# The four value products of an attention step side by side

## The reference, cut to what matters

```
def _attn(x, ln_w, ln_b, conv_w, attn_w, proj_w, n_head):   # B=4, T=512, C=128, 16 heads of 8
    h = layernorm(x); h = causal_depthwise_conv(h)
    q, k, v = split(h @ attn_w); q, k = rope(q), rope(k)
    scores = q @ k.T / sqrt(8)
    scores = where(causal, scores, -1e30)
    p = softmax(scores)
    return (p @ v) @ proj_w
```

## Time and profile before

| | |
|---|---|
| median of 3 runs | 2071.69 us (2069.89 to 2074.51) |
| the profiled execution | 2067.15 us, of which the span 2065.4 us |
| PE busy | 1799.8 us, 87% of the span |
| DVE, ACT, POOL busy | 1536.7, 1335.5 and 655.4 us |
| mean granted TensorE clock | 0.944 |
| value products, L1362 | 1024 records, first at 1032.9, last at 1908.2 us |

### The profile page before, as it was taken

How to read it: one execution, slowest core, us unless ns; L and a number is a source line. 1 busy time by engine, 2 the same in 40 slices (tenths; PEclk the granted TensorE clock), 3 DMA queues, 4 the chain that set the end, 5 groups by cost and what they waited for, 6 DMA issues and landing times.

```text
span 2065.4 us, 24716 instructions
## 1 busy us (share of the span) xinstructions
PE 1799.8 (87%) x8806; PEld 1111.0 (54%) x8806; DVE 1536.7 (74%) x2489; ACT 1335.5 (65%) x2121; POOL 655.4 (32%) x735
## 2 busy tenths in 40 slices
PE   8999798888988889997798889997577678988998
PEld 5888466665666657885233335783122233332786
DVE  6888687787877758888766654875999866764786
ACT  6999577676776688997356565555544445566554
POOL 1444211011110013444523321322699442233131
PEclk9999999999999989998799998998899879999999
DMA  3221000000000002220000000200000000000110
GB/s 102 76 78 49 19 19 18 1 18 19 19 18 1 11 11 84 75 69 31 0 1 1 1 1 9 85 21 0 11 3 33 0 1 1 1 1 1 57 56 21
DMA packets 23770, 52.89 MB, mean 26 GB/s; under 512 B 2336, under 2 KB 6816, under 8 KB 23648
## 3 DMA queue, kind: packets, MB, share of 16 engines
q1 hardware_dynamic: 23648, 51.30, 7.8%
HBM read 49.66 MB, written 1.64 MB: 25 GB/s over the span
## 4 chain that ended last, share of the span: by engine, by line
PE 60%; DVE 20%; ACT 15%; issue 3%; POOL 1%; DMA 1%; SPq 0%; POOLq 0%; DVEq 0%; ACTq 0%
PE ps L554 9%; PE ps L556 9%; PE ps L555 9%; PE ps L1362 5%; DVE arena L1986 5%; PE ps L1331 4%; PE ps L786 3%; PE ps L783 3%; DVE arena L1703 2%; PE ps L784 2%; ACT arena L1502 2%; PE ps L1320 2%; PE ps L1350 2%; ACT arena L1451 2%; DVE arena L1977 1%
## 5 line engine op out<-in xcount | busy, mean ns | idle before, releaser
L665 DVE TENSOR_TENSOR hid_lo<-arena,hid_hi 128x512 fp32r<-128x512 f32 x384 | 341.6, 902 | 67.5 <-ACT arena L614 65.5
L1703 DVE TENSOR_REDUCE arena<-ps 128x1 f32<-128x512 f32 (+3 forms) x352 | 219.2, 641 | 82.5 <-PE ps L1335 78.9
L1502 ACT ACTIVATE arena<-ps 128x1024 f32<-128x1024 f32 (+3 forms) x256 | 167.6, 703 | 120.9 <-PE ps L1350 120.6
L554 PE MATMUL ps<-x_hi,w_hi 128*128 128x512 f32 x512 | 208.1, 406 | 3.1 <-DVE arena L757 3.1
L556 PE MATMUL ps<-x_hi,w_lo 128*128 128x512 f32 x512 | 203.4, 397 | 0.0
L555 PE MATMUL ps<-x_lo,w_hi 128*128 128x512 f32 x512 | 203.2, 397 | 0.0
L611 ACT ACTIVATE hid_hi<-ps,wslot 128x512 fp32r<-128x512 f32 x256 | 177.3, 693 | 33.8 <-PE ps L556 6.4
L1616 POOL TENSOR_SCALAR_AFFINE_SELECT arena<-arena 128x256 f32<-128x256 f32 x256 | 108.0, 428 | 283.7 <-ACT arena L1502 281.5
L614 ACT ACTIVATE arena<-ps,wslot 128x512 f32<-128x512 f32 x256 | 175.1, 684 | 0.0
L1331 PE MATMUL ps<-arena 128*128 128x512 bf16 (+3 forms) x512 | 138.5, 328 | 41.0 <-DVE arena L1703 12.7
L635 POOL TENSOR_TENSOR x<-x,arena 128x512 f32<-128x512 f32 x64 | 108.4, 1698 | 146.1 <-DVE arena L626 146.1
(11 more groups left out here) (314 smaller groups left out, 4233.7 us busy)
## 6 DMA issues: line engine op xcount, KB each, us to landing
arena<-gates_dram SPq DMA_DIRECT2D x96, 256.0 KB, 3.6
wslot<-pack_a SPq DMA_DIRECT2D x16, 514.5 KB, 3.6
wslot<-pack_b SPq DMA_DIRECT2D x8, 900.5 KB, 4.6
wslot<-pack_c SPq DMA_DIRECT2D x8, 768.0 KB, 4.5
res<-x_in SPq DMA_DIRECT2D x4, 256.0 KB, 5.1
out_dram<-res SPq DMA_DIRECT2D x4, 256.0 KB, 2.8
con<-consts_dram SPq DMA_DIRECT2D x1, 559.0 KB, 4.0
bc_dram<-arena SPq DMA_DIRECT2D x1, 384.0 KB, 3.2
```

The costliest lines, as they stand in the source:

```text
L554: pe.matmul(ps[:, bank, :], w1, hi, start=start, stop=False)
L665: dve.tensor_tensor(hid_lo[item % 2][:, k, :], hid32[:, k, :], hid_hi[item % 2][:, k, :].bitcast(F32), ALU.subtract).then_inc(S["hid_ok"], 1)
L1502: act.activation(pt[:, u % NPT, :, 0:n], ps[:, 2 * r:2 * r + 2, 0:n], ACT.Exp, scale=SCALE).then_inc(S["exp_ok"], 1)
L1703: dve.tensor_reduce(neg_max[:, i, heads[0]:heads[-1] + 1:step], ps[:, bank, 0:len(heads) * keys].rearrange("p (m k) -> p m k", k=keys), AX ...
```

## The change

Before, a step ran: scores pair, first quarter of sides, scores pair, second quarter, value pair, third quarter, value pair, fourth quarter. Now the two value pairs stand together behind the second quarter, and the third and the fourth quarter of the sides follow. The wait for the first pair's selection is gone; all four products wait for the second's. Products, operands and the number of semaphore signals are the same.

```diff
-            def values(b, j, r):
+            def values(b, j):
                 q, g, k = q0 + b, j // TPB, j % TPB
-                if k == 0 and r == 0 and 4 * b + g:
+                if k == 0 and 4 * b + g:
                     pe.wait_ge(S["pvs_ok"], 4 * q + g)
-                pe.wait_ge(S["sel_ok"], 32 * q + 2 * j + r + 1)
-                if (b, j, r) == (2, 0, 0):
+                pe.wait_ge(S["sel_ok"], 32 * q + 2 * j + 2)
+                if (b, j) == (2, 0):
                     pe.wait_ge(S["pad_ok"], 2 * c["attn"] + 2)
-                for m in (2 * r, 2 * r + 1):
+                for m in range(4):
                     mm = pe.matmul(ps[32 * m:32 * m + 32, 4, k * P:SEQ], vc[b % 3][:, k, 4 * g + m, :],
                                    pt[:, (2 * j + m // 2) % NPT, m % 2, 0:SEQ - k * P], start=(k == 0),
                                    stop=(k == TPB - 1), skip_group_check=True)
-                if r:
-                    mm.then_inc(S["pv_mm"], 1)
+                mm.then_inc(S["pv_mm"], 1)
...
-                    for r in range(2):
-                        values(b, j, r)
-                        sides(2 + r)
+                    values(b, j)
+                    sides(2)
+                    sides(3)
```

## The result

The changed kernel takes 2049.14 us (median of 4, 2047.66 to 2054.99), the kernel before in the same comparison 2072.89 us: 23.8 us less, a ratio of 0.9886 with a 95% interval of 0.9864 to 0.9909. Forecast was 2045.2 us in a range of 2030 to 2062. The profiled execution took 2048.71 us with a span of 2047.0, 18.4 us under the profiled one of before.

What follows compares the result with a forecast made beforehand. PE was taken to set the pace where side work runs, with DVE two thirds loaded behind it. 29.8 - 0.3 - 3.0 = 26.5 us off 2067.15 gives 2040.6, plus 4.54 to the median: 2045.2 us, range 2030 to 2062.

Steps and rivals of the forecast that it cites:

- The price of four: Value products of a step: four together cost what two cost, so each second pair's 0.98, 0.77, 0.56 or 0.34 us is saved.
- The account of a batch: Steps 1 to 12 of batch 1, walked step by step: 4.97 us kept a batch, 29.8 us over six.
- The rules: Batch 1 walk: PE keeps order and spacing, uses wait for readers plus 0.05 us, readers keep their distance or queue.
- one DVE pause: Step 12: one of the two 0.67 us pauses that its value pairs put between DVE's reductions goes away.
- The rule on readers: Skill's warning that emptying PSUM may become the bottleneck: 29.8 us gained with the readers instead of 47.7 by PE alone.
- the ceiling: Twelve steps a batch with side work: 7.95 us saved if PE waited for nobody, 47.7 us over six batches.
- The clock: PE less dense, so two more falls of its granted clock: 3 us lost, bounds -3 to +9 us.
- The prediction's own sign of being wrong: Batches 0 to 2: the forecast is wrong if their granted clock falls below 0.95.
- the bound of +9 us: Upper bound of the loss to lower granted clock, for six more falls.
- Batch 3: Batch without side work: first value pair also waits for the second half's selection; 0.3 us lost, from nothing to 2 us.
- the wait in step 7: Batch 3: the second half's weight load waits 0.40 us for POOL; the first pair moves behind it, ending as before.
- the three terms: Gain of 29.8 us in six batches with side work, less 0.3 us in batch 3 and 3.0 us to the clock.

Runs made afterwards that it cites:

- e7: The changed kernel with two of the four value products of every step left out; 2045.60 us, ratio 0.9861 to the kernel before.
- e1: The changed kernel with the four heads' value products written to only two column groups of TensorE; 2088.65 us, ratio 1.0081 to the kernel before.
- e4: The changed kernel with row maxima taken over only the first quarter of each head's keys, so VectorE's reductions are shorter; 2019.18 us, ratio 0.9744.
- e9: The changed kernel with ScalarE's copies of transposed keys and queries cut to two of eight pairs for batches 2 and 3; 2029.38 us, run once.
- e6: The changed kernel plus unread products filling PE's idle time at the change from one batch to the next; 2044.47 us, ratio 0.9851.
- e11: The kernel before, old order, plus unread products filling PE's idle time between batches; 2072.26 us against 2072.61, ratio 0.9998.
- e8: The changed kernel run again unaltered, for a second profile and median; 2050.25 us, ratio 0.9889 to the kernel before.

## Why the prediction was right

**The price of four.** Right, and shown: 1.06 us for four, 1.05 for two (e7), 1.91 when they have two column groups (e1). The value products of steps 1 to 13 fell to half, and no instruction was added.

**The account of a batch.** Start of the value products, before and after, and the lead relative to step 1 (0.92 us there), beside the running sum of the prediction up to that step:

| step | before | after | lead measured | forecast |
|---|---|---|---|---|
| 2 | 1105.10 | 1103.32 | 0.86 | 0.77 |
| 3 | 1109.58 | 1107.47 | 1.19 | 1.13 |
| 5 | 1118.67 | 1116.02 | 1.73 | 1.70 |
| 7 | 1125.45 | 1121.82 | 2.71 | 2.56 |
| 8 | 1130.16 | 1126.54 | 2.70 | 2.44 |
| 10 | 1137.81 | 1132.68 | 4.21 | 3.93 |
| 13 | 1148.88 | 1142.65 | 5.31 | 4.97 |

The rules held (order kept, 0.05 us from reader to PE, a reader at its distance), nearly step by step: step 3 gave nothing, step 7 lost 0.01 us where 0.12 was said; the largest misses are step 5 (0.52 kept, 0.30 said) and steps 11 and 12 (0.70 kept, 0.47 said). The sum was 0.34 us too low. PE's idle time grew by 2.87 us, where about 3 was said, and batch 1 takes 59.2 us from start to start of its step 0 products, where 59 was said. In steps 10 to 13 one DVE pause is left of two, as foretold.

**What holds the rest.** 2.6 of 7.95 us a batch are not won. The waits name mostly reductions (1.8 of 2.9 us of new idle time), and e4 shows 1.0 us coming back without them; e9 shows 0.3 us for ScalarE's copies. Neither alone gives back what its waits show; that the next reader in turn then sets the pace is my reading. What both together would give was not tried, so most of the 2.6 us is put down to the readers by the waits alone.

**The rule on readers.** By the section "PSUM Bottleneck" of the Trainium skill's "TensorEngine Tiling (Array Packing)" the emptying of PSUM may become the bottleneck when TensorE gets faster. Here it holds in part: 67% of the ceiling was kept where 63% was foretold, and most of PE's new waits are for readers of PSUM (2.4 of 2.9 us).

**The clock.** More falls came, as said, but the term was too small and their places were only in part those foretold: four runs of value products a call are stretched by a fall (1.50 to 1.94 us), where two were before. At full clock steps 1 to 13 save 5.14 us in batch 0 and 5.31 in batches 1 and 2, 31.5 us over six batches (29.8 forecast). The two stretches got shorter by 12.0 and 12.2 us, so 7.3 us went elsewhere, where the sum had 3.0. Of these, 3.3 us lie inside steps 1 to 13, in two batches: batch 2 of the first call, with a fall at step 1, and batch 0 of the second, with falls at steps 1 and 8 (42.97 and 42.34 us at full clock):

```profile
1160.09:1203.77 43.68, 38.49 (x334) 16.59 (x335) 33.80 (x68) 26.61 (x39) 10.97 (x30) 0.98 0.00 1
1680.71:1725.59 44.88, 38.99 (x323) 15.94 (x324) 32.61 (x65) 26.13 (x38) 10.95 (x30) 0.93 0.01 1
```

The other 4.0 us went between steps 13 and 1. Both calls issue the same instructions in these stretches, and yet the falls stand at other steps in the second than in the first, so PE's lower density alone doesn't say where they come. The prediction's own sign of being wrong, a granted clock below 0.95 in batches 0 to 2, appeared in two of the six batches: 0.93 in batch 2 of the first call, and 0.88 in batch 0 of the second, shown at e6.

```profile
1153.79:1210.50 56.71, 48.36 (x412) 20.55 (x413) 38.28 (x79) 35.60 (x53) 15.76 (x42) 0.93 0.00 1
```

The mean of each stretch is 0.95. In the stretches the bound of +9 us covers the loss; over the whole of the two profiles it does not, 31.5 - 18.4 = 13.1 us.

**Batch 3.** I took 0.3 us of loss; it is 1.0 us shorter in the first call and 1.6 in the second. Steps 0 to 7, where the wait stands, take 19.59 us instead of 19.64, so the cost is nothing: the wait in step 7 (0.40 us at the second weight load) became one of 0.53 us before all four, with the run itself shorter, as said. The gain is in steps 8 to 11, 9.24 us at a granted clock of 1.00 instead of 10.46 at 0.84 in the first call: a fall that moved, and nothing that was foretold.

**What wasn't in the sum.** In the profiles 5.4 us of the gain are missing behind the second attention, at a clock of 0.94 instead of 0.97, 2.8 before the first and 0.2 between the two, in code that the change doesn't touch. The profile of e11 shows the slower end with the old order (and the fill), so it belongs to where the clock falls, not to the value products. Sum of the profiles: 24.2 + 2.6 (batch 3, both calls) - 8.4 = 18.4, as measured. The medians give 23.8 us; the profiled execution of before, 2067.15 us, is one of its fastest (2066.39 to 2082.67 over all sets), and which part of the other executions lacks these falls is not shown, since they have no profile.

**Luck.** In the attention 31.5 - 7.3 + 2.6 = 26.8 us were gained where 26.5 were forecast, but the three terms were off by +1.7, -4.3 and +2.9 us and nearly cancelled. The forecast put the profiled execution at 2040.6 us and it took 2048.71, 8.1 more; the 4.54 us from the profiled one to the median of before, added for the forecast of 2045.2, were 0.43 us after. So the median came within 3.9 us partly because that difference shrank.

## What to carry to other kernels

Value products in different column groups of TensorE cost next to nothing beside each other here (1.06 us for four, 1.05 for two), so look whether all of them are issued in one run; two runs of two cost twice. Before adding up such savings, walk through one period and ask at each double-buffered bank which reader comes next: here a third of the ceiling was not won. And when PE becomes less busy, read its granted clock again, stretch by stretch; work put into its idle time is worth a try, with the same edit of the old kernel beside it, but look in the trace whether the falls that vanish are those next to it.

## What the runs showed of the hardware

With idle-time products the changed kernel was 5.8 us faster, although PE's busy time in a stretch rose (147.4 us in e8, 149.2 in e6), at a granted clock of 0.98 instead of 0.95. One fall of 2.7 us vanished right behind them; others vanished where none stood. The falls of the clock come back at the same places in two profiles of one kernel, but move with small edits elsewhere: the same last part took 156.9, 162.3, 162.3 and 161.2 us. That is more than many edits are worth, and only a comparison of the stretches themselves keeps it out.
